# Attention, FFN, attention and gated FFN in one kernel: softmax and norms of the first token group in halves, and down products of two tiles ahead of the second group's value-output product

## The chip, the cores and the metric

The kernel runs on one core of one Trainium2 chip. The metric is the device time of one execution in microseconds; three executions of the kernel before were timed. The change lies in the last quarter of the execution, from 292 us on.

## The reference, cut to what matters

There are 1024 tokens of 256 numbers (8 tiles of 128 tokens). Two attention and FFN layers come first; the change touches the second attention layer and the last, routed FFN. `x2` below is the sum after the first FFN.

```
scores = layernorm(x2) * (q k^T / 8) + masks        # per token 256 numbers
x3 = x2 + softmax(scores)
xn = layernorm(x3)
h  = r1 * (n1-weighted xn) @ (wv wo) + xn + bias     # r1: the rms of the first norm
h2 = r2 * h                                          # r2: rms of h, from sum of squares
g  = silu(h2 @ w_gate) * (h2 @ w_up)                 # 704 wide
y  = xn + h + g @ w_down, taken where the router says so, otherwise xn
out = x3 + y
```

Fp32 operands of the gate, up and down products are split into a rounded high part and the rest, so that each product is three matmuls (high x high, high x rest, rest x high).

## The kernel before, in words

Each engine has one instruction list written out by hand, and semaphores order them. All work of the last layers is done for tokens in two groups: tiles 0 to 3 and tiles 4 to 7.

For each group the chain is this. PE contracts the first FFN's second product into a bank (`contract(t)`, 16 bf16 matmuls, L1832). DVE adds it to `xs` (`x2_tile`, L1183) and takes statistics. DVE forms the gated scores (`gate_scores`, L1195), a Newton step finishes 1/sqrt (`newton`, L887, which waits for a `pow` of POOL, L441), and masks are added (`mask_scores`, L1201). `largest` (L1210) is one reduce over the group's four tiles. ACT exponentiates (`softmax`, L791), DVE sums (`x3_sums`, L1214), takes statistics and three small steps for r1 (`x3_statistics`, L1223), waits for POOL, and gives ACT the bias and scale of the norm (`shift3_ready`). ACT writes the four normed tiles (`norm_rows`, L802). PE transposes them (`turn_norm`, L1843, which writes banks 4 and 5 for group one, 6 and 7 for group two), ACT copies them out (`turned_copy`, L567), and PE multiplies them with the value-output matrix, tile t into bank t (`attend`, L1846, fp32). DVE builds h (`h_tile`, L1242), ACT squares and sums (`h_square_sum`, L820), POOL takes another power, DVE scales (`h2_tiles`, L1255), PE transposes, ACT and DVE make the high and low parts (`tail_copy`, L808; `tail_lows`, L1316).

Then come six gate steps for the group. `gate_high(n)` (L1881) and `gate_low(n)` (L1893) are 8 and 4 matmuls of 512 columns (4 and 2 in the last), into two banks that `GATE_PAIR` names. ACT applies `silus(n)` (L830), DVE multiplies (`gated(n)`, L1333, which frees the banks), ACT rounds (`high_part(n)`, L837), DVE subtracts (`low_part(n)`, L1340). `GATED_FIRST` says how many `gated` must be done before a gate step may write its banks: one for step 4, two for step 5. `down` (L1901) has for each tile 6 parts of three matmuls; part ft waits for `low_part(ft)`. `DOWN_BANK` names the bank per tile: tiles 0 and 1 use banks 4 and 5, which are also those of `attend` for tiles 4 and 5.

The order on PE around the change: contract 4 and 5, 16 filler matmuls (`keep_busy`, L1741), the transposes and `attend` of group one, contract 6 and 7, 10 fillers, the transposes of h2 and six gate steps of group one. Then `turn_norm(1)`, `attend(1)`, `down_two(0)` (L1912), the transposes of group two's h2, down of tiles 2 and 3, and the six gate steps and four downs of group two.

On POOL the list is: powers 4, 5, 6, then four adds `shifted_tiles(0)` (L540), powers 7 to 10, `shifted_tiles(1)`, power 11, and two large adds (L562) after h2 of all tiles.

SP takes part only in the output: a DMA for each tile when `y_ready` comes.

## Time and profile before

| what | us |
|---|---|
| median of three executions | 384.93 |
| lowest and highest of them | 383.13, 386.03 |
| the profiled execution, its own time | 386.52 |
| the span of its trace | 384.4 |
| mean granted clock of TensorE in it | 0.991 of full |

The span begins and ends with the trace. The profiled execution's own time is 2.1 us longer than its span. Durations below come from this one execution. A time such as 311.00 is counted from the start of the span.

### The profile page before, as it was taken

How to read it: one execution, taken by the hardware profiler on the slowest of the kernel's cores; microseconds unless marked ns; L12 is line 12 of the kernel's file. 1: busy time of each engine (PE TensorE's matmuls, PEld its weight loads, DVE VectorE, ACT ScalarE, POOL GpSimd, SP SyncE). 2: the span in 40 equal slices, each digit the busy share in tenths (PEclk: the TensorE clock that was granted, in tenths of full speed). 3: DMA queues.
4: the chain of work that ended last, by engine and by line, in shares of the span. 5: the costliest groups of instructions: out<-in, count | busy, mean ns of one | idle time of the engine just before them, and what ended most of it. 6: DMA issues, size and time to landing. Idle time of an engine off the chain costs nothing.

```text
span 384.4 us, 6374 instructions
## 1 busy us (share of the span) xinstructions
PE 366.5 (95%) x2185; PEld 267.3 (70%) x2185; DVE 295.8 (77%) x674; ACT 208.5 (54%) x555; POOL 174.5 (45%) x163
## 2 busy tenths in 40 slices
PE   8799999999999999999999999998999789989996
PEld 8775676677676766776767677764556467879885
DVE  5698698698667886976697765578899967897773
ACT  1524476457546664765576494617974362582240
POOL 2454665476448645764665430671801232056100
PEclk9999999999999999999999999999999969999999
DMA  7639100300301103000004000400000000000001
GB/s 245 213 112 342 62 1 0 111 3 1 112 0 46 65 0 112 3 0 2 0 3 150 3 0 2 119 0 3 0 3 0 0 2 0 3 0 2 28 28 56
DMA packets 9087, 17.55 MB, mean 46 GB/s; under 512 B 2144, under 2 KB 6944, under 8 KB 8160
## 3 DMA queue, kind: packets, MB, share of 16 engines
q1 hardware_dynamic: 9056, 17.14, 13.3%
q8 instruction: 18, 0.29, 0.3%
q14 instruction: 13, 0.11, 0.1%
HBM read 16.09 MB, written 1.05 MB: 45 GB/s over the span
## 4 chain that ended last, share of the span: by engine, by line
PE 67%; DVE 14%; ACT 7%; POOL 6%; issue 3%; DMA 2%; SPq 0%; DVEq 0%; POOLq 0%
PE bank L1524 16%; PE bank L1595 7%; PE bank L1570 7%; PE bank L1586 6%; PE bank L1554 4%; PE bank L1539 3%; PE bank L1476 3%; PE bank L1616 2%; PE bank L1839 2%; DVE relu L1159 2%; PE bank L1443 2%; DMA blobs<-in_blob 2%; POOL prob L463 2%; PE bank L1851 2%; PE bank L1445 1%
## 5 line engine op out<-in xcount | busy, mean ns | idle before, releaser
L463 POOL TENSOR_TENSOR prob<-prob,rinv 128x512 f32<-128x512 f32 x64 | 65.9, 1041 | 74.4 <-DVE rinv L1023 74.4
L1524 PE MATMUL bank<-xnT,w 128*128 128x512 f32 x288 | 90.2, 434 | 1.7 <-DVE xnT L920 1.7
L621 ACT ACTIVATE prob<-bank,negmax 128x256 f32<-128x256 f32 x128 | 59.0, 478 | 29.5 <-DVE negmax L1017 29.5
L1017 DVE TENSOR_REDUCE negmax<-bank 128x2 f32<-128x512 f32 x64 | 40.8, 680 | 35.3 <-PE bank L1570 35.3
L1524 PEld LDWEIGHTS bank<-xnT,w 128*128 128x128 f32 x288 | 50.4, 189 | 19.5 <-issue 13.3
L631 ACT COPY probT<-bank 128x512 f32<-128x512 f32 x64 | 37.7, 589 | 22.8 <-PE bank L1586 22.8
L951 DVE TENSOR_TENSOR rot_up<-bank,cb 64x512 f32<-64x512 f32 x64 | 44.1, 689 | 1.6
L458 POOL TENSOR_TENSOR rot_low<-rot_low,rot_up 128x512 f32<-128x512 f32 x32 | 41.0, 1281 | 3.8 <-DVE rot_up L951 3.8
L1586 PE MATMUL bank<-ca,prob 128*128 128x128 f32 x256 | 39.4, 276 | 0.5 <-ACT probT L631 0.3
L1586 PEld LDWEIGHTS bank<-ca,prob 128*128 128x128 f32 x256 | 29.1, 140 | 13.8 <-issue 5.3
L443 POOL TENSOR_TENSOR c_y<-c_ve,minus_half 128x4 f32<-128x4 f32 (+1 forms) x9 | 9.8, 1086 | 61.2 <-DVE c_ve L901 45.5
L1570 PEld LDWEIGHTS bank<-ktmp,uT 64*128 64x128 f32 x256 | 23.4, 186 | 13.4 <-issue 11.3
L1570 PE MATMUL bank<-ktmp,uT 64*128 64x256 f32 x256 | 32.0, 389 | 0.0
L456 POOL TENSOR_TENSOR rot_z<-rot_z 128x512 f32<-128x512 f32 x16 | 21.1, 1322 | 23.8 <-DVE rot_z L951 23.8
L1595 PE MATMUL bank<-probT,kva 128*64 128x256 f32 x256 | 31.1, 384 | 0.5
L1616 PE MATMUL bank<-wkvo,cT 128*128 128x256 f32 x128 | 29.7, 381 | 0.0
L621 ACT ACTIVATION_READ_ACCUMULATOR prob<-bank,negmax 128x1 f32 x128 | 26.7, 209 | 0.0
L1595 PEld LDWEIGHTS bank<-probT,kva 128*64 128x64 f32 x256 | 17.7, 137 | 12.7 <-ACT probT L631 3.9
L1616 PEld LDWEIGHTS bank<-wkvo,cT 128*128 128x128 f32 x128 | 23.5, 190 | 3.9 <-issue 1.2
L946 DVE TENSOR_TENSOR rot_low<-bank,cb 128x512 f32<-128x512 f32 x32 | 21.9, 685 | 4.6 <-PE bank L1524 4.6
L636 ACT COPY cT<-bank 128x512 f32<-128x512 f32 x15 | 8.8, 585 | 28.4 <-PE bank L1595 28.4
L951 DVE TENSOR_TENSOR rot_z<-bank,cb 64x512 f32<-64x512 f32 x32 | 22.0, 688 | 0.4
(212 smaller groups left out, 706.8 us busy)
## 6 DMA issues: line engine op xcount, KB each, us to landing
blobs<-in_blob SPq DMA_DIRECT2D x7, 1024.0 KB, 4.9
xs<-in_x SPq DMA_DIRECT2D x2, 512.0 KB, 4.1
xn<-in_w_fc_t SPq DMA_DIRECT2D x1, 1024.0 KB, 4.9
ctxT<-in_w_proj_t SPq DMA_DIRECT2D x1, 1024.0 KB, 5.3
out<-qk SPq DMA_DIRECT2D x8, 128.0 KB, 1.7
cb<-in_const_b SPq DMA_DIRECT2D x1, 768.0 KB, 9.0
blobs<-in_w_gate SPq DMA_DIRECT2D x1, 704.0 KB, 5.2
blobs<-in_w_up SPq DMA_DIRECT2D x1, 704.0 KB, 6.5
```

Source lines behind the costliest of these rows:

```text
L458: pool.tensor_tensor(low[:, r, :], low[:, r, :], up[:, r, :], ALU.add).then_inc(joined, 1)
L463: pool.tensor_tensor(p[:], p[:], rinv[:, n % PROBS, :].unsqueeze(2).to_broadcast([P, 2, S]), ALU.mult).then_inc(normed, 1)
L621: ins = act.activation(prob[n % PROBS][:, st, :], pS[n % UNITS][:, st * S:(st + 1) * S], ACT.Exp, bias=negmax[:, n % UNITS, st:st + 1], ac ...
L631: act.copy(probT[n % UNITS][:].rearrange("p a s -> p (a s)"), pT[:]).then_inc(probsT_copied, 1)
L946: dve.tensor_tensor(tokens(rope_parts(m)[0]), tokens(src[:]), angles(cosq, r), ALU.mult)
L951: ins = dve.tensor_tensor(tokens(crossed[to:to + DC, :]), tokens(src[lo:lo + DC, :]), angles(sinq, r, lo, lo + DC), ALU.mult)
L1017: dve.tensor_reduce(negmax[:, n % UNITS, :], pS[n % UNITS][:].rearrange("p (a s) -> p a s", a=2), AX, ALU.max, negate=True).then_inc(max_r ...
L1524: ins = pe.matmul(q_bank(m)[:], w[a][:, k, r * P:(r + 1) * P], x[b][:, k, c * CH:(c + 1) * CH], start=(i == 0), stop=(i == 5))
L1570: ins = pe.matmul(pS[2 * a + h][:, st * S:(st + 1) * S], uT[g % 2][lo:hi, at:at + P], ktmp[lo:hi, b * S:(b + 1) * S], start=True, stop=True)
L1586: ins = pe.transpose(pT[:, lt * S + st * P:lt * S + (st + 1) * P], prob[n % PROBS][:, st, lt * P:(lt + 1) * P], ident)
L1595: ins = pe.matmul(o[h * DC:(h + 1) * DC, :], kva[:, 2 * b + lt, :], probT[2 * a + h][:, lt, :], start=(lt == 0), stop=(lt == 1))
L1616: return pe.matmul(bank[OUT_BANK[t // 2]][:, t % 2 * D:(t % 2 + 1) * D], cT[:, f, t * P:(t + 1) * P], wkvo[:, f, :], start=(f == 0 and t % ...
```

## The change

The softmax of each group is cut in two halves of two tiles: `mask_scores`, `largest`, `softmax` and `x3_sums` now take a number from 0 to 3, and `x3_sums` includes the row statistics of its two tiles. The last steps of `x3_statistics` are a function of their own, `x3_squares`, called later. In group one DVE itself writes the normed tiles 0 and 1 (new semaphore `first_normed`, and `norm_of(t)` names who made a tile), and ACT tiles 2 and 3. `turn_norm` waits for each tile by itself.

The order of DVE's other work around these is new: h8 steps, `x2_tile(4)` to `x2_tile(7)`, `tail_lows(0)`. On ACT `softmax(3)` stands between `silus(0)` and `silus(1)`, and `norm_rows(1)` stands after `silus(5)` and ahead of `high_part(4)`. The fillers are 25, 19 and 4, and the ten ahead of the turned h2 are gone. Contract 5 and 6 follow `attend(0)`, and contract 7 follows the high part of gate step 0. `down_two(0)` comes ahead of `attend(1)`, in banks 3 and 1, and `turn_norm(1)` stands within it, after the first five parts of tile 0. Down of tile 2 and four parts of tile 3 come ahead of the turned h2. The three gate steps 6, 7 and 8 wait for `down_taken` 1, 2 and 4.

```diff
-DOWN_BANK = (4, 5, 0, 1, 4, 5, 6, 7)
+DOWN_BANK = (3, 1, 4, 5, 4, 5, 6, 7)
...
+        first_normed = sem("first_normed")
...
+        def norm_of(t):
+
+            return (first_normed, t + 1) if t < 2 else (norm_ready, NT + t - 1)
...
-                    pool.wait_ge(norm_ready, NT + t + 1)
+                    pool.wait_ge(*norm_of(t))
...
-            pool.wait_ge(norm_ready, 2 * NT)
+            pool.wait_ge(*norm_of(NT - 1))
...
-            def softmax(c):
-                act.wait_ge(gated_ready, c + 1)
-                for t in range(4 * c, 4 * c + 4):
+            def softmax(two):
+                act.wait_ge(gated_ready, two + 1)
+                for t in range(2 * two, 2 * two + 2):
...
             softmax(0)
+            softmax(1)
             rounded_top(5)
...
-                for t in range(4 * c, 4 * c + 4):
+                for t in range(2 if c == 0 else 4, 4 * c + 4):
...
             rounded_top(6)
-            rounded_top(7)
...
             for t in range(4):
                 h_square_sum(t)
+            rounded_top(7)
             tail_copy(0)
-            softmax(1)
+            softmax(2)
...
             silus(0)
+            softmax(3)
             silus(1)
             high_part(0)
             silus(2)
             high_part(1)
             silus(3)
-            norm_rows(1)
             high_part(2)
-            turned_copy(8, tailT, turned_copied, (2, 3))
             silus(4)
             high_part(3)
             silus(5)
+            norm_rows(1)
             high_part(4)
-            h_square_sum(4)
-            h_square_sum(5)
             high_part(5)
-            h_square_sum(6)
-            h_square_sum(7)
+            turned_copy(8, tailT, turned_copied, (2, 3))
+            for t in range(4, NT):
+                h_square_sum(t)
             tail_copy(1)
...
-            def mask_scores(gr):
-                lo, hi = groups[gr]
-                newton(4 + 4 * gr, rstd, lo, hi)
+            def mask_scores(two):
+                lo, hi = 2 * two, 2 * two + 2
...
+            newton(4, rstd, 0, half)
             mask_scores(0)
             largest(0)
+            mask_scores(1)
+            largest(1)
             h8_shared(4)
+            x3_sums(0)
+            in_order(x3_sums(1))
+            aggregate(5, 0, half)
             h8_halved(5)
-            h8_shared(5)
-            x3_sums(0)
-            x3_statistics(0)
-            x2_tile(4)
             newton(5, rstd, 0, half)
             dve.scalar_tensor_tensor(out=negmean[:, 0:half], in0=mv[:, 0:half, 0], scalar=-1.0, in1=rstd[:, 0:half],
                                      op0=ALU.mult, op1=ALU.mult).then_inc(shift3_ready, 1)
+            for t in range(2):
+                normalise(t).then_inc(first_normed, 1)
+            x3_squares(0)
+            h8_shared(5)
             h8_halved(6)
-            h8_shared(6)
-            x2_tile(5)
             dve.wait_ge(variance_ready, 6)
             newton(6, r1, 0, half, of=(c_q, c_y1))
+            h_tile(0)
+            x2_tile(4)
+            h_tile(1)
+            h_tile(2)
+            h_tile(3)
+            h8_shared(6)
+            h_square(0)
             h8_halved(7)
             h8_shared(7)
-            for t in range(half):
-                h_tile(t)
-            h_square(0)
-            x2_tile(6)
             dve.wait_ge(variance_ready, 7)
             newton(7, r2, 0, half)
             h2_tiles(0)
+            x2_tile(5)
...
+            tail_lows(0)
+            x2_tile(6)
             in_order(x2_tile(7))
             aggregate(8, half, NT)
             dve.wait_ge(qk_copied, 8)
             gate_scores(1)
-            mask_scores(1)
-            largest(1)
-            tail_lows(0)
-            x3_sums(1)
+            newton(8, rstd, half, NT)
+            mask_scores(2)
+            largest(2)
+            mask_scores(3)
+            largest(3)
+            x3_sums(2)
...
             gated(0)
-            x3_statistics(1)
+            in_order(x3_sums(3))
+            aggregate(9, half, NT)
+            x3_squares(1)
             gated(1)
...
             gated(4)
             low_part(3)
+            gated(5)
+            low_part(4)
+            low_part(5)
+            add_base(0)
             h_tile(4)
-            gated(5)
             h_tile(5)
-            low_part(4)
             h_tile(6)
             h_tile(7)
-            low_part(5)
+            add_base(1)
             h_square(1)
+            take(0)
+            take(1)
             dve.wait_ge(variance_ready, 11)
             newton(11, r2, half, NT)
             h2_tiles(1)
-            for t in range(half):
-                add_base(t)
+            add_base(2)
+            add_base(3)
             tail_lows(1)
-            for t in range(half):
-                take(t)
+            take(2)
+            take(3)
...
             def turn_norm(c):
-                turn(1, lambda t: xn[:, t, :], norm_ready, NT, (2 * c, 2 * c + 1))
+
+                for k in range(DK):
+                    for t in range(4):
+                        if k == 0:
+                            pe.wait_ge(*norm_of(4 * c + t))
+                        ins = pe.transpose(bank[4 + 2 * c + k][:, t * P:(t + 1) * P],
+                                           xn[:, 4 * c + t, k * P:(k + 1) * P], ident)
+                    ins.then_inc(turned, 1)
...
-            keep_busy(18, 1)
+            keep_busy(25, 1)
             contract(4)
-            contract(5)
-            keep_busy(16, 1)
+            keep_busy(19, 1)
             pe.wait_ge(qk_copied, 8)
             turn_norm(0)
+            keep_busy(4, 1)
             attend(0)
+            contract(5)
             contract(6)
-            contract(7)
 
             pe.wait_ge(wgu_low, 4)
-            keep_busy(10, 4)
             turn(2, atbuf, h2_ready, 0, (0, 1))
...
-                if n == 7:
-                    pe.wait_ge(down_taken, 4)
+                if n in (6, 7, 8):
+                    pe.wait_ge(down_taken, (1, 2, 4)[n - 6])
...
                 down(t, range(FT1 - 1))
+                if t == 0:
+                    pe.wait_ge(act_ready, 3)
+                    turn_norm(1)
+                    pe.wait_ge(act_ready, 5)
                 down(t + 1, range(FT1 - 1))
...
             pe.wait_ge(h_ready, 4)
+            gate_high(0)
+            contract(7)
+            gate_high(1)
             pe.wait_ge(x2_ready, NT)
-            for n in range(3):
-                gate_high(n)
+            gate_high(2)
...
-            pe.wait_ge(act_ready, 3)
-            turn_norm(1)
-            pe.wait_ge(act_ready, 4)
+            down_two(0)
             attend(1)
+            pe.wait_ge(h_ready, 5)
+            down(2, range(FT1)).then_inc(down_ready, 1)
             pe.wait_ge(h_ready, 6)
-            down_two(0)
+            down(3, range(4))
             turn(2, atbuf, h2_ready, 0, (2, 3))
-            for t in (2, 3):
-                down(t, range(FT1)).then_inc(down_ready, 1)
+            down(3, range(4, FT1)).then_inc(down_ready, 1)
```

## Rows read from the trace of the kernel before

**Rows 1.** The page, granted clock of TensorE in 40 equal slices of the span
```profile
PEclk9999999999999999999999999999999969999999
```

**Rows 2.** Windows: length, busy (x) of PE, PEld, DVE, ACT, POOL; granted clock, DMA, GB/s
```profile
298.42:300.08 1.66, 0.00 (x1) 0.03 (x1) 1.66 (x3) 0.77 (x3) 0.00 (x0) 1.00 0.00 0
...
307.19:311.00 3.81, 1.72 (x9) 0.94 (x8) 3.71 (x8) 3.20 (x7) 2.99 (x5) 0.92 0.02 4
311.00:317.60 6.60, 6.60 (x16) 5.23 (x17) 3.19 (x6) 3.49 (x8) 0.30 (x1) 0.53 0.00 0
...
324.74:339.87 15.13, 15.13 (x66) 12.34 (x67) 13.43 (x41) 9.16 (x21) 3.40 (x5) 1.00 0.01 2
...
345.60:356.24 10.64, 10.64 (x80) 9.76 (x80) 7.36 (x21) 3.15 (x9) 6.49 (x3) 1.00 0.01 2
```

**Rows 3.** Timeline of PE: start us, us, line, operation, tiles, [idle before <-releaser]
```profile
300.08 3.65 PE L1839 MATMUL bank<-wpr,tail_all 128*128 128x256 bf16 x32 [1.66 <-DVE tail_all L1273]
...
311.00 6.78 PE L1851 MATMUL bank<-cb,tailT 128*128 128x256 f32 x16 [0.72 <-ACT tailT L571]
...
341.72 3.69 PE L1851 MATMUL bank<-cb,tailT 128*128 128x256 f32 x16 [0.82 <-ACT tailT L571]
```

**Rows 4.** Timeline of ACT, first and second group
```profile
299.31 0.51 ACT L794 ACTIVATE xn<-xn,c_m 128x256 f32<-128x256 f32 x1 [4.24 <-DVE c_m L1212]
...
307.38 2.08 ACT L805 ACTIVATE xn<-xs,negmean,rstd 128x256 f32<-128x256 f32 x4 [5.05 <-DVE negmean L1300]
...
328.82 0.51 ACT L794 ACTIVATE xn<-xn,c_m 128x256 f32<-128x256 f32 x1 [3.65 <-DVE c_m L1212]
...
330.71 0.19 ACT L794 ACTIVATION_READ_ACCUMULATOR xn<-xn,c_m 128x1 f32 x1
330.92 1.28 ACT L835 ACT_TABLE_LOAD   x1
332.21 1.09 ACT L835 ACTIVATE tail_all<-bank 128x512 f32<-128x512 f32 x2
...
337.72 2.07 ACT L805 ACTIVATE xn<-xs,negmean,rstd 128x256 f32<-128x256 f32 x4
```

**Rows 5.** Timeline of DVE, first and second group
```profile
298.06 1.22 DVE L1212 TENSOR_REDUCE c_m<-xn 128x4 f32<-128x1024 f32 x1
...
301.63 1.67 DVE L1220 SCALAR_TENSOR_TENSOR xs<-xn,c_r,xs 128x256 f32<-128x256 f32 x4
303.22 1.40 DVE L1228 BATCH_NORM_STATS2 stats<-xs 128x6 f32<-128x256 f32 x4
...
305.07 0.17 DVE L901 TENSOR_SCALAR c_ve<-mv 128x4 f32<-128x4 f32 x1
...
307.19 0.16 DVE L1300 SCALAR_TENSOR_TENSOR negmean<-mv,rstd 128x4 f32<-128x4 f32 x1
...
322.06 0.48 DVE L1186 SCALAR_TENSOR_TENSOR xs<-bank,sc,xs 128x256 f32<-128x256 f32 x1
...
337.18 0.16 DVE L1378 SCALAR_TENSOR_TENSOR negmean<-mv,rstd 128x4 f32<-128x4 f32 x1
...
339.43 3.28 DVE L1345 TENSOR_TENSOR gated_lo<-tail_all,gated_hi 128x512 fp32r<-128x512 f32 x3
...
343.24 0.68 DVE L1345 TENSOR_TENSOR gated_lo<-tail_all,gated_hi 128x512 fp32r<-128x512 f32 x1
...
349.48 1.14 DVE L1260 TENSOR_SCALAR at_rows<-h_rows,r 128x256 f32<-128x256 f32 x4
350.54 1.42 DVE L1349 TENSOR_TENSOR h_rows<-h_rows,xs 128x256 f32<-128x256 f32 x4
```

**Rows 6.** Timeline of POOL, second group
```profile
336.52 1.01 POOL L443 TENSOR_TENSOR c_y<-c_q,minus_half 128x4 f32<-128x4 f32 x1
338.45 3.71 POOL L545 TENSOR_TENSOR at_rows<-xn,cb 128x256 f32<-128x256 f32 x4 [0.92 <-ACT xn L805]
...
350.77 5.80 POOL L562 TENSOR_TENSOR qk<-xs,xn 128x1024 f32<-128x1024 f32 x2 [1.99 <-DVE at_rows L1260]
```

More of the change, by code:

```diff
@@ L1208, in mask_scores, with largest, x3_sums @@
                 in_order(ins)
-            def largest(gr):
-                lo, hi = groups[gr]
+            def largest(two):
+                lo, hi = 2 * two, 2 * two + 2
                 dve.tensor_reduce(c_m[:, lo:hi], xn[:, lo:hi, :], AX, ALU.max, negate=True).then_inc(gated_ready, 1)
-            def x3_sums(gr):
-                lo, hi = groups[gr]
+            def x3_sums(two):
+                lo, hi = 2 * two, 2 * two + 2
                 dve.wait_ge(soft_ready, hi)
@@ L1221, in x3_sums @@
                                              in1=xs[:, t, :], op0=ALU.mult, op1=ALU.add).then_inc(x3_ready, 1)
-            def x3_statistics(gr):
-                lo, hi = groups[gr]
                 for t in range(lo, hi):
@@ L1228, in x3_statistics, with x3_squares @@
                     ins = dve.bn_stats(stats[:, t, :], xs[:, t, :])
-                in_order(ins)
-                aggregate(5 + 4 * gr, lo, hi)
+                return ins
+            def x3_squares(gr):
+                lo, hi = groups[gr]
                 in_order(dve.reciprocal(c_q[:, lo:hi], c_ve[:, lo:hi]))
@@ L1233, in x3_statistics @@
                 dve.tensor_scalar(c_q[:, lo:hi], c_q[:, lo:hi], 1e-6, None, ALU.add).then_inc(variance_ready, 1)
-            def norm_tiles(gr):
-                lo, hi = groups[gr]
-                newton(5 + 4 * gr, rstd, lo, hi)
-                for t in range(lo, hi):
-                    normalise(t).then_inc(norm_ready, 1)
             def h_tile(t):
```

## The prediction, made before the change was run

> **What bounds the kernel now.** I read the page first. Its clock line dips in one slice only, to 6 tenths, about 310 us in [rows 1]. The windows around the change show where. From 307.19 to 311.00 PE is busy 1.72 of 3.81 us, with transposes that wait for ACT, and then the granted clock is 0.53 for the 6.60 us of attend(0) [rows 2], that is mostly the lower of the two levels, 1.2 of 2.4 GHz. The timeline of PE gives the price: the same 16 matmul records take 6.78 us for group one and 3.69 for group two [rows 3], so 3.1 us are the clock's. Third, the chain of group one, in the timelines of DVE and ACT: the reduce at 298.06, exp at 299.31, the variance at 305.07, the norm's bias at 307.19, four norm rows to 309.46, and after transposes and copies attend at 311.00 [rows 3 to 5]. Last, the second half of the stage: PE has no gap from 324.74 to 339.87 (66 matmuls in 15.13 us, 0.229 each) [rows 2], waits 0.82 before attend(1) [rows 3], and has none from 345.60 to 356.24 (80 instructions) [rows 2]. There PE is the bound, and ACT and DVE are kept just ahead of it.
>
> **Group one, softmax and norm in halves.** A reduce of 1024 elements takes 1.22 [rows 5], one of half the size about 0.65. With two masks ahead of it (0.9) the first half reaches ACT at 297.95 instead of 299.31, the second at 299.4, and its exps end at 300.5. DVE then needs 1.8 per half (reciprocal 0.2; sums and statistics are 1.67 and 1.40 for four tiles [rows 5], half of that is 1.5, and 0.1 of wait), from 300.0 to 303.6, and 0.4 for the aggregates: the variance at 304.05 instead of 305.07. x2_tile(4), which sat under POOL's power and held the newton back by 0.3, is gone from there, so the bias ends at 306.0 instead of 307.35. Two tiles on DVE and two on ACT (0.52 each, as 2.08 for four [rows 4]) are done at 307.1 instead of 309.46. From there to attend it was 1.54 (309.46 to 311.00); attend(0) starts at 308.7, **2.3 us earlier**.
>
> **The clock in attend(0).** The fillers now run to 306.0, four more cover the copies, and the thin stretch is 1.9 us (306.0 to 307.9) instead of 3.81. An idle stretch of 1.66 us at 298.42 did not bring the clock down [rows 2]. I take attend at 3.45 to its last start and the next work at 312.2, instead of 317.7: **5.5 earlier** in all. If it drops again, 3.1 come back.
>
> **Until the first gate step.** Contract 5 and 6 take 3.65 for the two [rows 3], to 315.9. Beside them h of tile 3 comes at 312.9, ACT's sum at 313.55, power (1.01, [rows 6]), newton 0.6 behind two h8 steps (1.3), and four h2 tiles 1.14 [rows 5], to 316.7. The last transposes wait for it, and gate step 0 starts at about 317.6 instead of 324.74: 7.1 earlier, of which 2.2 are the ten fillers. But contract 7 (1.8) comes after it, so x2_tile(7) runs at 321.9; before it was 322.06 [rows 5]. **The chain of group two starts no earlier**, only PE's gate steps do, by 5.3.
>
> **Group two, softmax around silu(0).** Before, the four exps end at 330.90, a table load takes 330.92 to 332.20, and the two silus follow [rows 4]. It is the only load of this stage. The new order is exp, exp, silu, exp, exp, silu. By what this row shows each change of function pays 1.28, so two loads are added. Walked through: the first two exps start at 327.3 (halves, 1.5 earlier), load, silu(0) 329.7, load, exps of tiles 6 and 7 from 331.5 to 332.55, load, silu(1) at 333.9, where it was 332.8. DVE's last sums, statistics and variance end at 335.05, gated(1) at 336.35, the bias at 337.0 against 337.34 [rows 5]. Gate step 5 needs gated(1). PE is through step 4 at 334.0 and idles 2.5 us. Both ends for the loads: if the two functions shared a table nothing is added and the end comes 1.5 earlier; three loads, no more, is the other end.
>
> The Trainium skill speaks against this edit (ScalarE: Activation LUTs, "What ACT_TABLE_LOAD costs" and the rule on batching by set): do all calls of one table set before the other, since a switch is 1283 ns plus a drain of about 1380, 2.66 in all. The trace agrees on the load and shows no drain: the read-out ends at 330.90 and the load starts at 330.92 [rows 4]. By the page's 2.66 the two added switches would make the time some 2.8 us longer than the one I give.
>
> **Group two, norm rows behind silu(5).** ACT is in order: high_part(1) waits for gated(1), high_part(2) for gated(2) (338.35, behind the two newtons), silu(4), high_part(3), silu(5) at 340.0, norm rows 340.5 to 342.5; they ran at 337.72 before [rows 4], with their bias no later than now. high_part(4) is queued behind them, to 343.1, and low_part(4) behind that. Down needs the low parts one by one: part 0 at 339.6, part 4 at 343.8. POOL's four adds (3.71, [rows 6]) now lie at 341.1 to 344.5, beside the lows; before, three lows beside them took 3.28, 1.1 each, against 0.68 alone [rows 5], so I add 0.45: part 4 starts at 344.3. PE ends step 5 at 337.8 and until 344.3 has four down parts of 0.36 (five parts and turns, 80 instructions in 10.64 us, give 0.13 for a matmul [rows 2]), so 5.1 us of idle, with the 2.5 above 7.6. Before it waited some 1.2 there: 0.82 for attend(1) [rows 3] and a little ahead of the downs.
>
> **From there to the end.** PE from 344.7, behind part 4: transposes 1.0, five parts of tile 1 1.8, two last parts 0.9, attend(1) 3.45: to 351.8. The old order had attend(1) and both downs done at 350.3. Then down of tile 2 and two thirds of tile 3 (3.7) to 355.5. The last attend tile, h (0.5), square sum (0.65), power (1.0), newton (0.7), h2 (1.14) need 4.3 from 351.8, so the transposes wait for 356.1 (the old chain took 5.1, from attend's end at 345.41 to 350.54 [rows 3, 5]). Transposes 0.6, two parts 0.8, gate step 6 at about 357.8, where it was 356.24. gate step 8 waits 0.3 for gated(6), and the rest is PE's as before: **1.9 us later** at the end with the clock full. POOL's 5.80 [rows 6] now lies beside the router's reductions of DVE, ahead of gated(6), which step 8 needs; four adds of DVE beside it took the usual 1.42 [rows 5, 6], so I take nothing, with 1.5 us as the other end (the slowing of the lows).
>
> **The clock in group two.** From 334.0 to 344.3 PE would be busy 2.8 of 10.3 us, thinner and longer than the stretch that brought the clock down before [rows 2]. I expect it to fall at 340 to 344 and to stay low for the transposes, tile 1's parts and much of attend(1). Before, the clock stayed low for 6.3 us of dense work, at a price of 3.1 [rows 2, 3]. This is the upper bound; the lower is 0, if the bursts of down hold it. I take 2.4, nearer to the row, since the fall may come before the dense work starts.
>
> **Sum.** As a ledger of PE: gate step 0 7.1 earlier, contract 7 behind it +1.8, step 4's wait for gated(0) +0.5, the two idle stretches +7.6, the old waits -1.2 to -1.5, the transposes' wait for h2 +0.4 more than before, gated(6) +0.3: between +2.0 and +2.3 in the roundest numbers, +1.9 in the walk by times, which I keep. With +2.4 for the clock it is +4.3 on the profiled execution's own time of 386.52: **390.8 us**. The median of the runs is 384.93, 1.6 below the profiled one. A kernel before with a full clock in attend(0) would be at 383.4 (386.52 less 3.1), and the lowest run is 383.13, so I think that the runs differ by how much of that dip each has.
>
> **Rivals.**
> - *Same waits, full clock in group two*: 388.5. For it: down's parts are spread over the stretch. Against: 1.72 busy of 3.81 was not enough before [rows 2]. 0.22.
> - *Not slower: the order pays.* The one mechanism is attend(1). If the norm rows and high parts come in time for PE to do turn_norm(1) inside down 0 by about 341, the downs fill the wait for h2, the downs of tile 2 and part of 3 (3.7) lie beside the chain from attend to h2, and step 6 starts at 352 to 355.5 instead of 356.24: 382.5 to 386. It decides at low_part(4): up to 341.3 it pays, beyond it costs one for one. For it: gate steps are 5 us ahead. Against: loads and ACT's order. 0.22.
> - *The clock falls in attend(0) too*: group two's chain starts 3.1 later and so does all: 394. For it: transposes still wait for each tile. 0.08.
> - *The skill's rule on the switch's drain holds here*: about 393.6. The row shows no drain. The rule is in the Trainium skill, ScalarE: Activation LUTs. 0.03.
> - *Faster by more*, all waits gone and clock full: under 381. 0.05.
>
> My forecast, waits and a low clock in group two, has 0.40.
>
> **How the numbers follow.** Faster or slower by over 1% (what can be told from no change here) means below 381.1 or above 388.8. Slower: 0.40, 0.08, 0.03 and half of the first rival (388.5 lies at the bound), 0.62. Within 1%: the other half, 0.20 of the second, 0.31. Faster: 0.07. The range goes from the second rival's middle, 384.0, to the attend(0) case, 394.5; the forecast's own is 389 to 392.
>
> **What would show it.** Three table loads in this stage; silu(1) at about 333.9; PE idle near 334 to 336.4 and 338 to 339.6; attend(0) at 3.7 us, at a start near 308.7; norm rows of group two from 340.5; attend(1) near 348, its length above 4.5 us with a granted clock near 0.5 before it; gate step 6 at 358 to 360. The prediction is wrong if attend(1) starts before 344 or step 6 before 356, or if the added loads aren't there.

## The result, and the profile after

The changed kernel takes 392.25 us (390.56 to 393.01, 6 runs), the kernel before 385.16 beside it (383.13 to 386.33, 6 runs): a ratio of 1.0183, 95% interval 1.0149 to 1.0216. It is slower, as forecast. The time lies in the stated range of 384.0 to 394.5, just above the forecast's own 389 to 392. The profiled execution has 392.04 us of its own and a span of 390.3, against 386.52 and 384.4.

The start of the changed stretch is not at the same place in each execution. The first aggregate of group one (DVE's BATCH_NORM_AGGREGATE, a step that both kernels do alike, just ahead of what changes) is at 293.53 before and 293.20 after; over all kernels of this study it lies from 292.41 to 295.00. Times "from the aggregate" below are differences from that row in the same trace, so that this shift drops out.

The page of after, granted clock in 40 slices; it answers to [rows 1]:
```profile
PEclk9999999999999999999999999999999999869999
```
The dip around 310 us is gone, and one of two slices has come, between 332 and 351 us. Windows of after, columns as in [rows 2]:
```profile
333.98:336.71 2.73, 0.47 (x3) 0.04 (x1) 2.56 (x13) 2.00 (x5) 1.18 (x2) 1.00 0.00 0
336.71:338.50 1.79, 1.79 (x6) 1.05 (x6) 1.29 (x8) 1.10 (x2) 0.81 (x1) 0.83 0.00 0
338.50:340.15 1.65, 0.16 (x1) 0.00 (x0) 1.65 (x4) 1.21 (x3) 0.00 (x0) 0.50 0.00 0
340.15:345.06 4.91, 3.30 (x13) 2.71 (x13) 4.29 (x7) 4.10 (x8) 3.12 (x4) 0.50 0.00 0
345.06:347.40 2.34, 2.34 (x11) 2.34 (x12) 1.41 (x2) 0.44 (x1) 0.53 (x1) 0.50 0.00 0
347.40:348.20 0.80, 0.80 (x6) 0.80 (x5) 0.00 (x0) 0.53 (x2) 0.00 (x0) 0.54 0.00 0
348.20:350.60 2.40, 2.40 (x20) 2.14 (x18) 0.00 (x0) 0.20 (x1) 0.00 (x0) 1.00 0.00 0
```
PE is dense from 324.74 to 339.87 in the kernel before [rows 2]. Here it is busy 0.47 of 2.73 us, then 0.16 of 1.65 and 3.30 of 4.91. The clock falls in the second of these windows and is full again from 348.2. The timeline of PE, after:
```profile
308.26 3.72 PE L1872 MATMUL bank<-cb,tailT 128*128 128x256 f32 x16
...
316.36 1.46 PE L1452 MATMUL bank<-ca,at_rows 128*128 128x128 f32 x8 [0.78 <-DVE at_rows L1256]
...
336.71 0.50 PE L1910 MATMUL bank<-tail_hi,wgu_high 128*128 128x512 f32 x1 [2.27 <-DVE tail_all L1345]
...
340.15 0.58 PE L1457 MATMUL bank<-wd_high,gated_hi 128*128 128x256 f32 x1 [1.49 <-DVE gated_lo L1353]
...
345.06 0.58 PE L1457 MATMUL bank<-wd_high,gated_hi 128*128 128x256 f32 x1 [1.49 <-DVE gated_lo L1353]
...
350.61 3.72 PE L1872 MATMUL bank<-cb,tailT 128*128 128x256 f32 x16
...
367.57 0.50 PE L1910 MATMUL bank<-tail_hi,wgu_high 128*128 128x512 f32 x1 [1.66 <-DVE tail_all L1345]
```
attend(0) has its full clock (3.72 for 6.78, [rows 3]). The three waits in the middle are for gated(1), low_part(0) and low_part(4). attend(1) starts at 350.61 instead of 341.72 [rows 3]. The last line is gate step 8. The timeline of ACT, after, beside [rows 4]:
```profile
328.75 1.28 ACT L841 ACT_TABLE_LOAD   x1
330.05 0.60 ACT L841 ACTIVATE tail_all<-bank 128x512 f32<-128x512 f32 x1
330.67 1.28 ACT L799 ACT_TABLE_LOAD   x1
...
333.07 1.28 ACT L841 ACT_TABLE_LOAD   x1
334.37 0.60 ACT L841 ACTIVATE tail_all<-bank 128x512 f32<-128x512 f32 x1
...
340.58 0.59 ACT L841 ACTIVATE tail_all<-bank 64x512 f32<-64x512 f32 x1
341.20 2.07 ACT L811 ACTIVATE xn<-xs,negmean,rstd 128x256 f32<-128x256 f32 x4
343.18 1.12 ACT L849 CAST gated_hi<-tail_all 128x512 fp32r<-128x512 f32 x2
```
Three loads in place of one, and the norm rows behind silu(5), at 341.20 instead of 337.72. The timelines of DVE and, in the last two lines, of POOL, after, beside [rows 5, 6]:
```profile
322.20 0.48 DVE L1191 SCALAR_TENSOR_TENSOR xs<-bank,sc,xs 128x256 f32<-128x256 f32 x1 [1.79 <-PE bank L1853]
...
343.81 2.32 DVE L1353 TENSOR_TENSOR gated_lo<-tail_all,gated_hi 128x512 fp32r<-128x512 f32 x2 [0.59 <-ACT gated_hi L849]
...
361.67 2.42 DVE L1363 SCALAR_TENSOR_TENSOR ctxT<-xn,wr 128x256 f32<-128x256 f32 x1
...
364.03 0.41 DVE L1363 SCALAR_TENSOR_TENSOR ctxT<-xn,wr 128x256 f32<-128x256 f32 x1
...
341.94 3.65 POOL L550 TENSOR_TENSOR at_rows<-xn,cb 128x256 f32<-128x256 f32 x4 [4.43 <-ACT xn L811]
...
358.68 5.12 POOL L567 TENSOR_TENSOR qk<-xs,xn 128x1024 f32<-128x1024 f32 x2 [1.99 <-DVE at_rows L1256]
```
x2_tile(7) is at 322.20, where it was 322.06: the chain of group two is not earlier. The router's first product takes 2.42 us where its neighbours take 0.41, while POOL's two adds run, and gated(6) is queued behind it.

Where the time went, from the aggregate (before, after): attend(0) 17.47, 15.06; gate step 0 31.21, 25.05; x2_tile(7) 28.53, 29.00; attend(1) 48.19, 57.41; gate step 6 62.71, 66.99; end 90.87, 97.10. So 6.2 us of PE's lead at gate step 0 turn into 4.3 of delay at gate step 6, and the tail (from there to the end) adds 1.9.

### The profile page after: what moved, and what is told of

The parts are those of the page before. It is cut to its first block, busy times and chain, and to the rows that moved or that the text cites. A ratio compares the mean times of both kernels' runs of the same rounds, so it can differ in the third digit from the quotient of the medians.

```text
span 390.3 us, 6384 instructions
## 1 busy us (share of the span) xinstructions
PE 368.7 (94%) x2184; PEld 267.8 (69%) x2189; DVE 298.9 (77%) x680; ACT 210.6 (54%) x555; POOL 174.4 (45%) x163
## 4 chain that ended last, share of the span: by engine, by line
PE 64%; DVE 15%; POOL 7%; ACT 7%; issue 4%; DMA 2%; SPq 0%; DVEq 0%; POOLq 0%
PE bank L1538 16%; PE bank L1609 7%; PE bank L1584 7%; PE bank L1600 6%; PE bank L1568 4%; PE bank L1553 3%; PE bank L1490 3%; PE bank L1630 2%; PE bank L1853 2%; DVE relu L1164 2%; POOL c_y L448 2%; PE bank L1457 2%; DMA blobs<-in_blob 2%; POOL prob L468 2%; PE bank L1497 1%
```

## The experiments

Three theories stood at first. The loads and the late norm rows on ACT hold PE (mine). Or the order of the down products costs by itself. Or a part of the loss has to do with POOL's adds. The rival to all was that the halves of group one lose as well. The first four kernels (e1 to e4) vary the changed kernel, the next four take the change apart, the last four test what was then left. Each has the kernel before measured beside it: its median was 385.71 over 25 runs beside e5 to e8, and 385.07 to 385.93 beside the others. A ratio with its 95% interval comes from the single runs and is not exactly the quotient of the two medians (e1: 1.0207, where the medians give 1.0183).

**One load (e1).** softmax(3) directly behind softmax(2) on ACT, so one load as before.
```diff
             softmax(2)
+            softmax(3)
...
             silus(0)
-            softmax(3)
             silus(1)
```


> Beside the changed kernel (392.2 us): softmax(3) directly behind softmax(2), so one table load instead of three. If the two added loads are on the path: silu(1) ends near 333 instead of 335.0, PE's wait ahead of gate step 5 falls from 2.3 us to about 0.8, and the end comes 1.4 us earlier, 390.8. If the granted clock falls because of that thin stretch it stays full now, 1.5 more: 389.3. If the cost is in the place of the downs alone: within 0.4 of 392.2.

Measured: 392.98 us, ratio 1.0207 (1.0158 to 1.0256), no better than the change. PE's waits, e1:
```profile
332.23 0.50 PE L1910 MATMUL bank<-tail_hi,wgu_high 128*128 128x512 f32 x1 [1.69 <-DVE tail_all L1345]
335.70 0.50 PE L1910 MATMUL bank<-tail_hi,wgu_high 128*128 128x512 f32 x1 [0.46 <-DVE tail_all L1345]
339.14 0.39 PE L1457 MATMUL bank<-wd_high,gated_hi 128*128 128x256 f32 x1 [1.78 <-DVE gated_lo L1353]
...
344.05 0.38 PE L1457 MATMUL bank<-wd_high,gated_hi 128*128 128x256 f32 x1 [1.89 <-DVE gated_lo L1353]
```
The wait moved from gate step 5 to step 4; down part 0 starts 46.63 from the aggregate (46.95 in the change). In this place the two loads are worth 0.3 us. That is nearest to the third of the expectations, the place of the downs, though 0.8 above the changed kernel and not within 0.4. This profile has the clock at full throughout (0.998), which prices the dip: from down part 0 to gate step 6 it takes 18.61 us, the change 20.04, in the same order of work. The dip costs 1.4. It comes and goes: the other three of e1's four runs have mean clocks of 0.981 to 0.990.

**Norm rows earlier on ACT (e2).** Behind silu(3), as before; PE's order as in the change.
```diff
             silus(3)
+            norm_rows(1)
             high_part(2)
...
             silus(5)
-            norm_rows(1)
             high_part(4)
```


> Beside the changed kernel (392.2 us): norm_rows(1) ahead of high_part(2), behind silus(3), as in the kernel before; the loads stay. If high_part(4) was held up by the norm rows and by what stands around them: low_part(4) ends near 343 instead of 344.9, down of tile 0 is through near 343.5, attend(1) starts 1.5 to 2 us earlier, end 390.4. If ACT's four norm rows only change places with the casts and the low parts of tiles' parts 2 and 3 now hold down up: within 0.5 of 392.2.

Measured: 392.82, ratio 1.0195 (1.0155 to 1.0235): no gain. The rows run at 336.91 instead of 341.20, but PE has no use for them, because turn_norm(1) stands behind down part 4. POOL's shifts now lie beside the first lows: the three of DVE take 3.27 instead of 1.88, and each of the five down parts waits 0.4 to 0.8.

**POOL's base adds earlier (e3).** They need only x3 and the norms, so they go ahead of the power of h.
```diff
-            powers(11, 1, c_ve, c_y)
             pool.wait_ge(*norm_of(NT - 1))
-            pool.wait_ge(h2_ready, NT)
             for gr in range(2):
...
+            powers(11, 1, c_ve, c_y)
```


> Beside the changed kernel (392.2 us): POOL's two large adds ahead of power 11, as soon as the norm rows are there, instead of behind h2. If they block DVE's first router product (2.42 us instead of 0.42) and so gate step 8: the wait ahead of step 8 falls from 1.7 to below 0.3 us and the end is 1.5 earlier, 390.7. If DVE is late there for its own list: step 8 waits as before, 392.2. If the adds block DVE's low parts at their new place instead: above 392.5.

Measured: 389.93, ratio 1.0133 (1.0085 to 1.0181). Gate step 6 is where it was (67.05 from the aggregate, 66.99), gate step 8 no longer waits, and the end is at 95.20 instead of 97.10. The adds beside the router cost **1.9 us**. This comes from the traces, since the intervals of the two ratios overlap, and all of the traces agree: from gate step 6 to the end it takes 30.05 to 30.11 us in the change, e1, e2 and e8, where the adds lie beside the router's first product, and 28.10 to 28.19 in the kernel before and all others.

**All three (e4).** The edits of e1, e2 and e3 together.

> The three edits together. If each cost is on the path and they add up, 1.4 + 1.8 + 1.5 and 1.5 for a clock that then stays full: 386.0, still not below the kernel before (385.2). If they overlap: 387.5 to 389. If the order of downs ahead of attend(1) is good by itself once ACT keeps up: below 384.

Measured: 394.41, ratio 1.0228 (1.0185 to 1.027), the slowest of all. With the rows earlier, the base adds come earlier too and lie on the low parts. e4, POOL and then DVE:
```profile
343.44 5.57 POOL L564 TENSOR_TENSOR qk<-xs,xn 128x1024 f32<-128x1024 f32 x2
...
344.55 2.24 DVE L1351 TENSOR_TENSOR gated_lo<-tail_all,gated_hi 128x512 fp32r<-128x512 f32 x1
...
347.54 2.60 DVE L1351 TENSOR_TENSOR gated_lo<-tail_all,gated_hi 128x512 fp32r<-128x512 f32 x2
```
A low part takes 0.68 alone. The adds' block is not removed by moving them here, only laid on other work: the three together are 2.2 us slower than the change, where e3 alone is 2.3 faster. None of the expectations held.

**First part alone (e5).** Halves of both groups, fillers, contract 5 and 6 behind attend(0), and contract 7 behind gate step 0 as in the change; ACT's, DVE's and PE's order of group two's second half, the banks and the one load as before.
```diff
             softmax(2)
+            softmax(3)
...
-            down_two(0)
-            attend(1)
+            pe.wait_ge(act_ready, 3)
+            turn_norm(1)
+            pe.wait_ge(act_ready, 4)
+            attend(1)
+            pe.wait_ge(h_ready, 6)
+            down_two(0)
```


> The first part alone: halves in group one, its fillers, contract 7 behind the high part of gate step 0; from the norm of group two on in the order of the kernel before, with one table load and attend(1) ahead of the downs. Times from the first aggregate of group one: before 90.87 us to the end, changed 97.10. If group two's chain sets the end (x2_tile(7) at 28.5 before, 29.0 in the changed kernel): attend(1) stays near 48.2 and the end near 91, that is 386 to 387, and the 6 us by which gate step 0 is earlier become PE's waits. If PE's work sets it: the end near 86, 382. If the first part itself costs time: above 93.

Measured: 384.84, ratio 0.9988 (0.9961 to 1.0015). It loses nothing that can be told, and is a little better than the 386 to 387 of the first expectation. attend(1) starts 46.70 from the aggregate (48.19 before), but gate step 4 now waits 2.56 us for gated(0): PE's lead becomes a wait, since x2_tile(7) is no earlier (28.99). The trace of before has the clock's dip in attend(0), which delays its x2_tile(7) too. Without the dip (e7, below) the kernel before has x2_tile(7) at 25.48, attend(1) at 45.18 and the end at 87.84, so that e5, with 88.85, is 1.0 us behind it.

**Contract 7 ahead as well (e6).** On e5: contract 7 behind contract 6, in bank 3; the lows of the tail behind largest(3).
```diff
             contract(6)
+            contract(7)
...
             gate_high(0)
-            contract(7)
...
-            tail_lows(0)
             x2_tile(6)
...
             largest(3)
+            tail_lows(0)
```


> As the first part alone, with contract 7 ahead of gate step 0 (in bank 3) and x2_tile(7) ahead of tail_lows(0). If group two's chain sets the end: x2_tile(7) comes near 26 instead of 29, attend(1) near 45, and the end near 88, 383.5, below the kernel before (385.5). If PE's work sets it already: no gain over the first part alone.

Measured: 382.79, ratio 0.9953 (0.992 to 0.9986). x2_tile(7) is at 25.42 from the aggregate, 3.6 earlier than in e5, and the median is 2.05 lower. The trace does not show this gain: its execution is the slowest of e6's ten (385.58), and in it attend(1) is at 46.56 (e5 46.70) and the end at 88.70. The gate's low products wait for the tail's lows there, and they take 4.38 for eleven (2.79 at full clock, below), with a granted clock of 0.67 from 328.03 to 333.20. The five runs of e6 at a mean clock of 1.0 took 381.37 to 382.50. e6, PE:
```profile
328.03 0.50 PE L1920 MATMUL bank<-tail_lo,wgu_high 128*128 128x512 f32 x1 [1.82 <-DVE tail_lo L1326]
328.69 4.38 PE L1920 MATMUL bank<-tail_lo,wgu_high 128*128 128x512 f32 x11 [0.16 <-DVE tail_lo L1326]
```

**The kernel before with eight more fillers (e7),** four ahead of the turned tiles and four behind them, for the clock alone.
```diff
-            keep_busy(16, 1)
+            keep_busy(20, 1)
             pe.wait_ge(qk_copied, 8)
             turn_norm(0)
+            keep_busy(4, 1)
             attend(0)
```


> The kernel before with 4 more fillers ahead of the transposes and 4 between them and attend(0), nothing else. If the spread of its runs (383.1 to 386.9 at mean granted clocks of 0.999 to 0.986) is the fall in attend(0): every run near 383.2 with a clock of 0.998 or more, attend(0) in 3.7 us. If the transposes with their waits bring the clock down all the same: 385.5, as before.

Measured: 383.51, ratio 0.996 (0.9934 to 0.9985), attend(0) at 3.72 us and gate step 0 at 28.16 instead of 31.21. Six of ten runs had a mean clock of 1.0. The dip of the kernel before is worth some 1.5 us of its median, and it is what most of its spread is made of: of the 25 runs beside e5 to e8, those at a clock of 0.999 to 1.0 took 382.45 to 384.03, and those at 0.986 to 0.991 mostly 385.2 to 387.4.

**Second part alone (e8).** The kernel before with down_two(0) ahead of attend(1) and turn_norm(1) inside it, banks 3 and 1, the rows behind silu(5), the lows ahead of the h tiles; one load, no halves.
```diff
...
+            down_two(0)
-            pe.wait_ge(act_ready, 3)
-            turn_norm(1)
-            pe.wait_ge(act_ready, 4)
             attend(1)
-            pe.wait_ge(h_ready, 6)
-            down_two(0)
...
```


> The second part alone on the kernel before: downs of tiles 0 and 1 ahead of attend(1) in banks 3 and 1, norm rows behind silu(5), DVE's order of that stage; group one and the softmax of group two as before, one load. If down ahead of attend(1) costs by itself (norm rows near 341 to 343, low_part(4) near 344, attend(1) near 348.5 counted as in the kernel before): the end 3.5 us later, 1.9 of it ahead of gate step 6 and 1.6 the router's wait for POOL's adds, 389; 390.5 if the clock falls between. If it only cost because PE had run ahead of ACT and DVE in the changed kernel: within 1 us of 385.5.

Measured: 389.39, ratio 1.0134 (1.0079 to 1.0188). This part loses, by itself and with one load. Its profile has a full clock in attend(0), so e7's is the trace beside it: attend(1) starts 54.10 from the aggregate (e7 45.18), gate step 6 63.69 (59.68), end 93.75 (87.84). e8, PE:
```profile
339.25 0.39 PE L1445 MATMUL bank<-wd_high,gated_hi 128*128 128x256 f32 x1 [0.58 <-DVE gated_lo L1343]
...
341.75 0.38 PE L1445 MATMUL bank<-wd_high,gated_hi 128*128 128x256 f32 x1 [1.88 <-DVE gated_lo L1343]
...
347.35 3.72 PE L1853 MATMUL bank<-cb,tailT 128*128 128x256 f32 x16
```
What the order can win at best can now be estimated from these rows. From the start of attend(1) to gate step 6 it is 14.50 us in e7 and 14.02 in e5, with both downs in it, and 9.58 in the change, e1 and e2: 4.4 to 4.9 us less. And 36 products go ahead of attend(1), at 0.13 each (80 in 10.64 us, [rows 2]) 4.8. **By this estimate the order would win next to nothing even with no wait at all**, because PE had no gap behind attend(1) that the downs could have filled [rows 2]. No kernel here has the order and all its inputs in time, so it stays an estimate. All that it adds in waits is loss: attend(1) is 8.9 us later in e8 and may be 4.9.

**The two loads where the chain binds (e9).** On e5.
```diff
             silus(0)
+            softmax(3)
             silus(1)
...
             gated(0)
+            in_order(x3_sums(3))
+            aggregate(9, half, NT)
             x3_squares(1)
```


> The first part of the change alone (e5_first_part_alone, 0.9988 of the kernel before), and to it the two added table loads: the exps of tiles 6 and 7 stand between silu(0) and silu(1), their x3 sums behind gated(0), as in the changed kernel. Here group two's chain of norms binds the start of the value-output product again, so a load that lies on ScalarE ahead of it has nothing to hide behind. Theory 'a load costs its 1.28 us where the chain binds' (what I predicted for one of the two and rounded to 1.5 in all): the value-output product starts 1.3 to 2.8 us later from the first aggregate than e5's 46.70, and the time is 386.0 to 387.5. Theory 'the loads are nearly free, as e1_one_load seemed to show': value-output start within 0.5 of 46.70, time 384.5 to 385.5. If the loads cost as e1 said only because e1's chain did not bind, the first holds.

Measured: 386.5, ratio 1.003 (1.0001 to 1.0059), 1.7 us or 0.4% above e5. e9, PE:
```profile
342.12 3.69 PE L1870 MATMUL bank<-cb,tailT 128*128 128x256 f32 x16 [0.77 <-ACT tailT L576]
```
attend(1) is at 48.72 from the aggregate, 2.0 later than in e5. Two loads on the path cost 1.7, together with silu(0), which now stands ahead of the last exps; in the change itself (e1) the same move costs nothing that can be measured, since there the path runs over silu(5) and the norm rows.

**PE's order undone (e10).** The change with turn_norm(1) and attend(1) ahead of down_two(0), and the h tiles ahead of the two base sums that wait for it. ACT's order stays.
```diff
...
-            down_two(0)
+            pe.wait_ge(act_ready, 3)
+            turn_norm(1)
+            pe.wait_ge(act_ready, 5)
             attend(1)
+            down_two(0)
```


> The changed kernel with everything but the order of TensorE: turned normed tiles and value-output product of group two stand ahead of the down products of tiles 0 and 1 again, and VectorE's four h tiles and the h square ahead of the two base sums that wait for those products. Halves, banks 3 and 1, loads, ScalarE's order, the places of takes stay. Theory 'the order of the products is what costs': the value-output product starts 48 to 50 us from the first aggregate (changed kernel 57.41; e5 46.70 plus the added loads), the gate of step 6 at 61.5 to 63.5 (66.99), time 386 to 388. Rival 'ScalarE's order, which puts norm_rows(1) behind silu(5), and the low parts ahead of the h tiles cost as much': value-output start 52 or later, time 389.5 or more.

Measured: 392.03, ratio 1.0178 (1.0139 to 1.0218). The first theory fell: undoing PE's order alone gives nothing, and the rival's numbers came (attend(1) at 52.20). e10, PE and then ACT:
```profile
342.41 0.73 PE L1863 MATMUL bank<-ca,xn 128*128 128x128 f32 x2 [3.56 <-DVE tail_all L1345]
343.31 1.82 PE L1863 MATMUL bank<-ca,xn 128*128 128x128 f32 x6 [0.17 <-ACT xn L811]
345.89 5.84 PE L1872 MATMUL bank<-cb,tailT 128*128 128x256 f32 x16 [0.77 <-ACT tailT L576]
...
341.67 2.08 ACT L811 ACTIVATE xn<-xs,negmean,rstd 128x256 f32<-128x256 f32 x4
```
The wait is put down to DVE's tail_all; by the ACT line it is for the norm rows, the first of which ends just before the transposes start. Behind it the clock is down and attend(1) takes 5.84, which is 2.1 us more than the 3.72 of the change.

**Both orders undone (e12).** e10 with the norm rows behind silu(3) and the copies behind high_part(2).
```diff
             silus(3)
+            norm_rows(1)
             high_part(2)
+            turned_copy(8, tailT, turned_copied, (2, 3))
...
             silus(5)
-            norm_rows(1)
             high_part(4)
             high_part(5)
-            turned_copy(8, tailT, turned_copied, (2, 3))
```


> e10_value_output_first (1.0178) with ScalarE's order put back too: norm_rows(1) behind silu(3) instead of silu(5), the turned copies behind high_part(2); the value-output product waits for gated(3) as in the kernel before. In e10 the eight turned tiles stood 3.56 us for the norm rows, which stood behind silu(5) (ended 341.64, rows 341.67 to 343.75); in e9, with the old order, the rows ran at 337.90. Theory 'the late norm rows are what e10 still paid for': the turned tiles start 45.5 to 46.5 us from the first aggregate (e10 48.72, e9 45.74), the value-output product 48.5 to 49.5 (52.20), the gate of step 6 at 63 to 65, and the time is 386.5 to 388.5 (e9 386.5). Rival 'VectorE's order, low_part(3) to low_part(5) ahead of the h tiles, holds the h tiles anyway': turned tiles and product early, but the gate of step 6 at 66 or later and the time 390 or more.

Measured: 386.38, ratio 1.0004 (0.9975 to 1.0033). e12, ACT and then PE:
```profile
338.71 2.06 ACT L811 ACTIVATE xn<-xs,negmean,rstd 128x256 f32<-128x256 f32 x4
...
342.92 5.15 PE L1872 MATMUL bank<-cb,tailT 128*128 128x256 f32 x16 [0.77 <-ACT tailT L576]
```
attend(1) is at 48.71, as in e9. Halves, three loads, the banks and the low parts ahead of the h tiles all stay in this kernel, and it is as fast as the kernel before. The four corners, all with halves and three loads (e10 and e12 have the h tiles ahead of the base sums, which their order of PE demands; e2's copies stay behind the casts, where its order of PE holds them anyway):

| | ACT: rows behind silu(3) | ACT: rows behind silu(5) |
|---|---|---|
| PE: attend(1), then the downs | e12 1.0004 | e10 1.0178 |
| PE: the downs, then attend(1) | e2 1.0195 | the change 1.0183 |

Either order costs the whole 1.8% by itself, and the second one nothing more. That is why undoing one of them (e2, e10) did not help. That both losses have the same size is in part luck, because they are made of different terms. PE's order makes attend(1) late (58.51 in e2) and brings the 1.9 us beside the router. e10 has no such tail (28.19 from gate step 6 to the end); it pays for the late norm rows with 3.5 us ahead of attend(1) (52.20, e12 48.71) and by the clock behind them, with mean clocks of 0.974 to 0.991 in its six runs, where e12's twelve have 0.976 to 1.0.

**The lows earlier (e11).** e6 with tail_lows(0) between largest(2) and the next mask.
```diff
             largest(2)
+            tail_lows(0)
             mask_scores(3)
             largest(3)
-            tail_lows(0)
```


> e6_contract7_early (382.79, 0.9953) with the low parts of the tail between largest(2) and the second mask of group two, 1.5 us ahead of their place there, where the gate's low products waited 1.82 us for them and the clock fell behind that wait. If that wait took the clock: the wait shrinks to 0.3 to 0.6, no stretch at 0.5 around 329 to 333, and the time is 381.5 to 382.5, with runs at full clock in most executions. If the dip comes from elsewhere or the delay of the mask by 1.4 us on VectorE costs as much: 382.8 to 384. In either case under e5's 384.84.

Measured: **381.54 us, ratio 0.9905 (0.9869 to 0.9942)**, the fastest of all, under both kernels of this case. e11, PE:
```profile
325.89 0.50 PE L1920 MATMUL bank<-tail_lo,wgu_high 128*128 128x512 f32 x1 [0.33 <-DVE tail_lo L1326]
326.55 2.79 PE L1920 MATMUL bank<-tail_lo,wgu_high 128*128 128x512 f32 x11 [0.15 <-DVE tail_lo L1326]
```
The wait of 1.82 is 0.33, and the eleven products take 2.79 instead of 4.38, at full clock. attend(1) starts 44.41 from the aggregate, gate step 6 58.43 and the end is at 86.54. The kernel before has 48.19, 62.71 and 90.87, but with its clock's dip; against e7, which has none (45.18, 59.68, 87.84), e11 wins 1.3 us. By the ratios, 0.4 of its lead of 1% over the kernel before is what eight fillers also bring (e7, 0.9960), and its x2_tile(7), at 25.42, is no earlier than in e7.

## Why the prediction was right, and where not

Right in sign, and by most of its steps.
- *Group one.* attend(0) 2.3 earlier and at full clock, 5.5 in all: measured 2.41 and 3.72 instead of 6.78 us, 5.5 in all. Gate step 0 at 317.6: measured 318.25, 6.2 earlier from the aggregate instead of 7.1.
- *The chain of group two starts no earlier.* x2_tile(7) 321.9, measured 322.20. e5 and e6 show that this is what the first part's gain hangs on: 384.84 with it, 382.79 with contract 7 ahead. The row of 322.06 had the dip of attend(0) in it, which the comparison in the forecast did not take out; without the dip (e7) the old order has x2_tile(7) 3.5 us earlier than the change (25.48 and 29.00 from the aggregate).
- *Loads and norm rows.* silu(0) 329.7, silu(1) 333.9, rows 340.5, down part 0 339.6, part 4 344.3: measured 330.05, 334.37, 341.20, 340.15, 345.06, all 0.4 to 0.8 late. Three loads of 1.28 are there. Right in place, but wrong in weight: that without them "the end comes 1.5 earlier" holds where the chain of norms sets the start of attend(1) (e9, 1.7) and not for the changed kernel (e1, nothing). The Trainium skill counts a drain of some 1380 ns with each switch (ScalarE: Activation LUTs, "What ACT_TABLE_LOAD costs"). It is not in these rows: 328.75 and 1.28 end at 330.03, and silu(0) starts at 330.05.
- *The idle stretches.* 7.6 us were forecast; measured are 2.27, 1.49 and 4.91 less 3.30, or 5.4. The busy part is longer instead (5.7 of 11.1 us, forecast 2.8 of 10.3), as the clock was already down for the down parts.
- *The clock in group two.* It fell, as forecast, but at 338 instead of 340 to 344, and was back at 348.2, ahead of attend(1). "Its length above 4.5 us" is wrong, it took 3.72. The term of 2.4 us measured 1.4 (change against e1). In the other kernels the dip comes and goes between executions: the change's runs have mean clocks of 0.983 to 0.996.
- *Gate step 6.* 357.8 plus 2.4 for the clock is 360.2; measured 360.19. Two errors cancel there, the clock too dear by 1.0 and the walk too short by as much.
- *POOL beside the router.* **The step that failed**: "four adds of DVE beside it took the usual 1.42" and therefore "I take nothing, with 1.5 us as the other end". e3 prices it at 1.9. The row was of a start: DVE's adds began 0.2 us ahead of POOL's, and POOL's pair took 5.80 where it takes 5.12 in the change. The row never had the router's product beside POOL: it came at 356.69, after the pair's end at 356.57. In the change the router's product came 3 us after POOL's adds began, and waited.
- *The sum.* +4.3 was forecast; the span grew by 5.9, the own time by 5.5. From the aggregate it is 4.3 at gate step 6 (forecast 4.0) and 1.9 behind it (forecast 0.3), less 0.33 for the earlier start of the stretch: 5.9. The profiled execution of before was 1.4 above the median beside it, that of after is at its own (392.04 and 392.25), hence 7.1 between the medians. That the time was missed by only 1.5 us (390.8 and 392.25) is partly luck: the forecast added its 4.3 to the profiled execution and not to the median, which it knew to be 1.6 lower, and the growth was missed by 2.8. The reading of the spread, a dip in attend(0) that some executions have, held (e7).
- *The rivals.* The one on the other side was to decide at low_part(4), "up to 341.3 it pays". The estimate under e8 corrects its worth: even in time the order gives back next to nothing, since 4.4 to 4.9 us come out of the stretch behind attend(1) and 4.8 go in ahead of it. The kernels here that reach its 382.5 or come nearest have contract 7 ahead and the old order (e11, e6); whether the new order could get there was not run.

What the forecast lacked is the interaction. It walked one kernel and added its waits up as if each stood alone; the runs show that PE's order and ACT's order each make attend(1) late, and the larger hides the other.

## What to carry to other kernels

Moving work ahead of a product pays only as much as the engine idles behind that product. Read that idle time first; here it was none, so the best case was about zero (an estimate, see e8) and every new wait a loss. When a lead on one engine is won, look at whether the other chain that meets it starts earlier too (contract 7), and take a reorder back on all engines at once before judging its parts. A short wait ahead of dense TensorE work cost twice here, in itself and by the clock: with 1.5 us less of one wait e11 has a ratio of 0.9905 against e6's 0.9953 (their intervals just overlap). The two traces, 2.2 us apart at the end, show more than that, since e6's is of its slowest run. And compare with a trace of before whose clock is in the same state: a dip in one of two traces passes for a gain of the other.

## What was not expected of the hardware

A DVE operation whose two inputs are both in SBUF can last about as long as a POOL add that is under way: the router's product 2.42 us for 0.41, low parts 2.24 for 0.68 and 2.60 for two, and the add that held them ended within 0.3 us of them in the first case (POOL's pair ends at 363.80, the product at 364.09). Two low parts beside four smaller POOL adds (3.65 for four) took 2.32. A DVE operation with one input in a PSUM bank (gated(5), tail_all<-bank) kept its 0.69 at 342.53 in the change, beside POOL's adds of 341.94. With the adds moved away (e3) the router's first product takes its 0.41 again, so the wait is due to them. That the two meet at the memory's port fits these rows; no run tested it by itself.
